# Out-degrees of a graph as a fourth product of the adjacency build, in place of a histogram of their own

## What is computed

```python
row = jnp.concatenate([edge_index[0], loop])          # edge_index = (src, dst)
deg = jax.ops.segment_sum(jnp.ones_like(row, dtype=embedding.dtype), row, num_segments=N)
deg_inv_sqrt = jnp.where(deg > 0, jax.lax.rsqrt(jnp.maximum(deg, 1.0)), 0.0)
norm = deg_inv_sqrt[row] * deg_inv_sqrt[col]
out = jax.ops.segment_sum(norm[:, None] * embedding[row], col, num_segments=N)
```

## Time and profile before

| | us |
|---|---|
| median of 3 runs | 6698.84 (6689.83 to 6706.6) |
| the profiled execution | 6690.94 |
| its span on the core | 6689.2 |
| PE, DVE, ACT, POOL busy | 5658.0, 4679.1, 1031.0, 1809.4 |
| mean granted clock of PE | 0.93 of full speed |

### The profile page before, as it was taken

The page is one execution under the profiler, slowest core; times in us unless marked ns, Lnnn a source line. Parts: engine busy times, 40 slices in busy tenths (PEclk is TensorE's granted clock), DMA queues, the critical chain, the costliest instruction groups (busy, mean ns, idle before and its releaser), DMA issues. The chain is left out here.

```text
span 6689.2 us, 122051 instructions
## 1 busy us (share of the span) xinstructions
PE 5658.0 (85%) x41983; PEld 3702.9 (55%) x41983; DVE 4679.1 (70%) x10318; ACT 1031.0 (15%) x1894; POOL 1809.4 (27%) x1887
## 2 busy tenths in 40 slices
PE   4398999999999688888888888874899959968896
PEld 3257999999999444444444444443555524433344
DVE  7789999999999788888888888868566650032003
ACT  0044444444444000000000000013000010000000
POOL 0011000000000477777777777720000002000200
PEclk5578999999999899999999999997999979989996
DMA  9555777777777433333333333340888737635862
GB/s 316 148 170 170 192 189 193 184 196 191 190 193 185 111 82 83 82 83 83 83 83 82 82 82 83 80 35 0 324 306 304 283 119 192 192 124 193 190 203 69
DMA packets 559193, 1028.57 MB, mean 154 GB/s; under 512 B 187721, under 2 KB 447710, under 8 KB 549578
## 3 DMA queue, kind: packets, MB, share of 16 engines
q1 hardware_dynamic: 486760, 872.14, 44.0%
q0 software_dynamic: 65392, 145.28, 9.7%
q10 hardware_dynamic: 6622, 6.38, 0.3%
HBM read 688.67 MB, written 387.65 MB: 161 GB/s over the span
## 5 line engine op out<-in xcount | busy, mean ns | idle before, releaser
L1272 POOL DMA_INDIRECT big<-typed_msgs,big x1712 | 1644.7, 961 | 2220.2 <-DMA big<-edge_fields 1729.8
L1319 PE MATMUL psum<-big 128*128 128x384 f32 x3424 | 1343.8, 515 | 331.0 <-DMA big<-typed_msgs,big 328.9
L1155 PE MATMUL psum<-big 128*128 128x98 bf16 x7936 | 1549.0, 272 | 49.2 <-DVE big L1137 38.2
L1156 PE MATMUL psum<-big 128*128 128x49 bf16 x7936 | 1535.7, 229 | 0.2 <-issue 0.2
L1157 PE MATMUL psum<-big 128*128 128x49 bf16 x7936 | 1534.8, 230 | 0.0
L1743 PE MATMUL psum<-big 128*128 128x512 bf16 (+1 forms) x4704 | 1003.1, 376 | 186.8 <-DMA big<-adj 186.8
L1319 PEld LDWEIGHTS psum<-big 128*128 128x128 f32 x3424 | 583.7, 190 | 756.6 <-DMA big<-typed_msgs,big 502.0
L1155 PEld LDWEIGHTS psum<-big 128*128 128x128 bf16 x7936 | 933.3, 118 | 104.1 <-DVE big L1137 78.3
L1156 PEld LDWEIGHTS psum<-big 128*128 128x128 bf16 x7936 | 945.1, 119 | 0.0
L1157 PEld LDWEIGHTS psum<-big 128*128 128x128 bf16 x7936 | 932.1, 117 | 0.3 <-issue 0.3
L1743 PEld LDWEIGHTS psum<-big 128*128 128x128 bf16 x4704 | 463.3, 99 | 721.9 <-DMA big<-adj 191.9
(11 more groups left out here) (294 smaller groups left out, 4630.4 us busy)
## 6 DMA issues: line engine op xcount, KB each, us to landing
wadj<-big SPq DMA_DIRECT2D x248, 784.0 KB, 13.0
big<-wadj SPq DMA_DIRECT2D x124, 1568.0 KB, 7.2
big<-adj SPq DMA_DIRECT2D x210, 896.0 KB, 4.7
adj<-big SPq DMA_DIRECT2D x62, 1568.0 KB, 5.3
big<-edge_feats SPq DMA_DIRECT2D x856, 64.0 KB
edge_feats<-in_edge_attr SPq DMA_DIRECT2D x1, 51562.5 KB, 163.2
big<-typed_msgs,big POOLq DMA_INDIRECT x1712
big<-edge_fields SPq DMA_DIRECT2D x856, 8.0 KB
```

The source lines that it names most:

```text
L1155: pe.matmul(to[:, 0:2 * NB], lo, hi_b[:, q, g, :, u], start=True, stop=False)
L1156: pe.matmul(to[:, NB:2 * NB], lo, w2_b[:, q, g, :, u], start=False, stop=False)
L1272: pool.indirect_dma_start(out=got4[:, h, u, :], out_offset=None, in_=typed_rows, in_offset=bass.IndirectOffsetOnAxis(ap=fld4i[:, h, u, IDX ...
L1319: last = pe.matmul(ps[h][:, 0:T * P], got4[:, h, u, :], hot4[:, h, u, :], start=(u == 0), stop=(u == U - 1))
```

## The change

The 101 batches of source histograms are removed from DVE and PE. In the build, each tile gets a fourth product, `lo.T @ hi` with 49 columns, added over all 7936 tiles into one PSUM area (`sources`, bank 7); after the last batch DVE copies it to `outdeg`. The one-hots of the build now lie tile by tile with neighbouring columns, 50 wide in place of 49 (`NE`), compared in runs of two: for this every value of the table is written twice (`tabs` and `slot_tabs` double), and a new ramp `line` is made by two iotas of POOL. PSUM areas of the build are halved to 8 tiles, and PE and ACT hand over after each half batch (four copies a batch instead of two). The destination histogram keeps its layout.

```diff
+NE = NB + NB % 2
-        slot_tabs = nc.dram_tensor("slot_tabs", (GB * P, 5 * SLOTS), BF16, kind="Internal").ap()
+        slot_tabs = nc.dram_tensor("slot_tabs", (GB * P, 2 * 5 * SLOTS), BF16, kind="Internal").ap()
...
+                pool.iota(line[:, 0:P], pattern=[[1, P]], base=0, channel_multiplier=0,
+                          allow_small_or_imprecise_dtypes=True)
+                pool.iota(line[:, P:P + NE], pattern=[[1, NE]], base=1, channel_multiplier=0,
+                          allow_small_or_imprecise_dtypes=True)
...
-                def outs(j0, j1):
-                    for j in range(j0, j1):
-                        hist_hot(dve, sloc, sbkt, HB + j, j * TT, (HB + j) % 2)
-                outs(0, AHEAD)
...
-                    link(dve.tensor_tensor(rest, w, part[0], ALU.subtract))
-                    link(dve.tensor_copy(part[1], rest))
-                    dve.tensor_tensor(part[2], rest, part[1], ALU.subtract).then_inc(s_slot_w, 1)
+                    link(dve.tensor_tensor(rest, w, part[0][:, :, 0], ALU.subtract))
+                    link(dve.tensor_copy(part[1], rest2))
+                    dve.tensor_tensor(part[2], rest2, part[1], ALU.subtract).then_inc(s_slot_w, 1)
...
-                        outs(*shares[n])
...
-                dve.wait_ge(s_hist_mm, 2 * HB)
-                link(dve.tensor_copy(outdeg, out_count))
...
-                    act.copy(tabs[:, k, 0:3, :], ps[k][:, 0:3 * SLOTS].rearrange("p (r g) -> p r g", r=3)).then_inc(s_slot_e, 1)
+                    act.copy(tabs[:, k, 0:3, :, :].rearrange("p r g c -> p (r g) c"),
+                             ps[k][:, 0:3 * SLOTS].unsqueeze(2).to_broadcast([P, 3 * SLOTS, 2])).then_inc(s_slot_e, 1)
...
+        def in_pairs(hot):
+            return hot.rearrange("p t (c r) -> p t c r", r=2)
+        def ramp_to(c0, n):
+            return line[:, c0:c0 + n].rearrange("p (c r) -> p c r", r=2).unsqueeze(1).to_broadcast([P, TT, n // 2, 2])
+        def along_slots(pairs, n):
+            return pairs.unsqueeze(2).to_broadcast([P, TT, n // 2, 2])
...
-                            at_least(dve, s_mm_b, n - 1)
-                            hi = hi_b[:, q, :, 0:NB, :]
-                            dve.tensor_tensor(hi, ramps(1, NB + 1), along_t(sbk, NB), ALU.is_equal).then_inc(s_hi_b, 1)
-                            dve.tensor_tensor(lo_b[:, q, :, :, :], ramps(0, P), along_t(sl, P), ALU.is_equal)
+                            at_least(dve, s_mm_b, n * 2 - 2)
+                            hi = in_pairs(hi_b[:, q, :, 0:NE])
+                            dve.tensor_tensor(hi, ramp_to(P, NE), along_slots(sbk, NE), ALU.is_equal).then_inc(s_hi_b, 1)
+                            dve.tensor_tensor(in_pairs(lo_b[:, q, :, :]), ramp_to(0, P), along_slots(sl, P), ALU.is_equal)
...
+                dve.wait_ge(s_mm_b, 2 * NBATCH)
+                dve.tensor_copy(outdeg, sources).then_inc(s_clear, 1)
...
-                            at_least(pe, s_adj_e, n - 1)
-                            for t in range(TT):
-                                to = made_in(q)[:, t, :]
-                                g, u = t // TU, t % TU
-                                lo = lo_b[:, q, g, :, u]
-                                pe.matmul(to[:, 0:2 * NB], lo, hi_b[:, q, g, :, u], start=True, stop=False)
-                                pe.matmul(to[:, NB:2 * NB], lo, w2_b[:, q, g, :, u], start=False, stop=False)
-                                last = pe.matmul(to[:, NB:2 * NB], lo, w3_b[:, q, g, :, u], start=False, stop=True)
-                            last.then_inc(s_mm_b, 1)
+                            for h in range(2):
+                                at_least(pe, s_adj_e, n * 2 + (h - 1))
+                                for t in range(h * HT, (h + 1) * HT):
+                                    to = made_in(h)[:, t % HT, :]
+                                    lo = lo_b[:, q, t, :]
+                                    pe.matmul(sources, lo, hi_b[:, q, t, 0:NB],
+                                              start=isinstance(n, int) and n == 0 and t == 0,
+                                              stop=isinstance(n, int) and n == NBATCH - 1 and t == TT - 1)
+                                    pe.matmul(to[:, 0:2 * NE], lo, hi_b[:, q, t, :], start=True, stop=False)
+                                    pe.matmul(to[:, NE:2 * NE], lo, w2_b[:, q, t, :], start=False, stop=False)
+                                    last = pe.matmul(to[:, NE:2 * NE], lo, w3_b[:, q, t, :], start=False, stop=True)
+                                last.then_inc(s_mm_b, 1)
```

More of the change, by code:

```diff
@@ L182, in build @@
         ramp = sb("ramp", P * TU, BF16)
+        line = sb("line", P + NE, BF16)
         big_words = (nc.sbuf_bytes_remaining // 4) // 16 * 16 - 64
@@ L337, in build @@
         in_count = ps[5][:, 0:NB]
-        out_count = ps[5][:, 64:64 + NB]
         with nc.Block() as block:
@@ L847, in build @@
         w_rest, at = cut(at, 2 * SLOTS)
-        tabs, at = cut(at, 2 * 5 * SLOTS // 2)
-        tabs = tabs.bitcast(BF16).rearrange("p (k r g) -> p k r g", k=2, r=5)
+        tabs, at = cut(at, 2 * 5 * SLOTS)
+        tabs = tabs.bitcast(BF16).rearrange("p (k r g c) -> p k r g c", k=2, r=5, c=2)
         same, at = cut(at, JB)
@@ L880, in slots_here @@
                 eng.wait_ge(s_took[(n - JB) % GR], 16 * ((n - JB) // GR + 1))
-        AHEAD = 44
-        shares = [(AHEAD + (HB - AHEAD) * n // GB, AHEAD + (HB - AHEAD) * (n + 1) // GB) for n in range(GB)]
         with nc.Block() as block:
@@ L1028, in _ @@
             def _(pe):
-                def outs(j0, j1):
-                    for j in range(j0, j1):
-                        hist_sum(pe, out_count, HB + j, (HB + j) % 2, opens=j == 0, closes=j == HB - 1)
                 def turn(b):
@@ L1054, in _ @@
                         message(n - 1)
-                    outs(*shares[n])
-        tab, at = cut(0, 2 * 5 * SLOTS // 2)
-        tab = tab.bitcast(BF16).rearrange("p (k r g) -> p k r g", k=2, r=5)
+        tab, at = cut(0, 2 * 5 * SLOTS)
+        tab = tab.bitcast(BF16).rearrange("p (k r g c) -> p k r g c", k=2, r=5, c=2)
         def hots(at, n):
             c, at = cut(at, 2 * n * TT // 2)
-            return c.bitcast(BF16).rearrange("p (k g c t) -> p k g c t", k=2, g=TG, t=TU), at
+            return c.bitcast(BF16).rearrange("p (k t c) -> p k t c", k=2, t=TT), at
         lo_b, at = hots(at, P)
-        hi_b, at = hots(at, 2 * NB)
-        w2_b, at = hots(at, NB)
-        w3_b, at = hots(at, NB)
+        hi_b, at = hots(at, 2 * NE)
+        w2_b, at = hots(at, NE)
+        w3_b, at = hots(at, NE)
+        def in_pairs(hot):
[4 more added lines that the diff above has]
+            return pairs.unsqueeze(2).to_broadcast([P, TT, n // 2, 2])
         adj_st, at = cut(at, 2 * AROW // 2)
@@ L1082, in build @@
         NBATCH = GB * BATCHES
+        HT = TT // 2
         def block_pairs(eng, body):
@@ L1091, in made_in @@
         def made_in(q):
-            return psum[:, q * 2048:(q + 1) * 2048].rearrange("p (t c) -> p t c", c=P)
+            return psum[:, q * 1024:(q + 1) * 1024].rearrange("p (t c) -> p t c", c=P)
+        sources = ps[7][:, 0:NB]
         with nc.Block() as block:
@@ L1167, in body @@
                         for b in range(BATCHES):
-                            act.wait_ge(s_mm_b, i * (2 * BATCHES) + (k * BATCHES + b + 1))
-                            act.copy(adj_st[:, k, :, b * TT:(b + 1) * TT],
-                                     made_in(b % 2)[:, :, 0:NB].rearrange("p t s -> p s t"))
-                            act.copy(wadj_st[:, k, b // 2, :, b % 2 * TT:(b % 2 + 1) * TT],
-                                     made_in(b % 2)[:, :, NB:2 * NB].rearrange("p t s -> p s t")).then_inc(s_adj_e, 1)
+                            for h in range(2):
+                                act.wait_ge(s_mm_b, i * (4 * BATCHES) + (k * (2 * BATCHES) + 2 * b + h + 1))
+                                c0 = b * TT + h * HT
+                                act.copy(adj_st[:, k, :, c0:c0 + HT], made_in(h)[:, :, 0:NB].rearrange("p t s -> p s t"))
+                                act.copy(wadj_st[:, k, b // 2, :, c0 % 32:c0 % 32 + HT],
+                                         made_in(h)[:, :, NE:NE + NB].rearrange("p t s -> p s t")).then_inc(s_adj_e, 1)
                 block_pairs(act, body)
```

21 lines of the change are left out of this document (11 added, 10 removed).

## The result

The changed kernel takes 7044.74 us (median of 4 runs, 7038.75 to 7049.9) beside 6697.33 us of the kernel before (4 runs): a ratio of 1.0518, 95% interval 1.05 to 1.0536. I had forecast 6566 us and given "slower" 0.15. The profiled execution took 7041.01 us, its span is 7039.2 us, 350 us above that of before.

| | before | after | forecast |
|---|---|---|---|
| ACT's first pick of a chunk | 329.71 | 329.24 | near 329 |
| build starts (DVE clears PSUM) | 572.25 | 560.38 | near 528 |
| build ends (before: DVE's last operation; after: copy of the out-degrees) | 2194.08 | 2538.13 | near 2061 |
| length of the build | 1621.8 | 1977.8 | 1533 |

What follows compares the result with a forecast made beforehand. In the build, half of (DVE + PE + 0.16 us) set the batch pace; after the change, DVE alone would. 6690.9 - 86 (build) - 47 (slot stage) = 6558, median 7.9 above: 6566 us, range 6520 to 6685.

Steps and rivals of the forecast that it cites:

- "slower": Chance of 0.15 that the changed kernel takes longer than the one before: D, E or a full clock drop.
- The change in the build, PE: Build: a tile's 249 neighbouring columns take PE 125 ns (bounds 105 to 244), a batch 2.23 us.
- The rest of the build's sum: Build: DVE sets the pace at 3.09 us a batch instead of 3.263, -86 us (bounds -61 to -98); ACT's copies hidden.
- rival B: Build: PE idles a third of the time and its clock falls; 6735 us if always, 6645 if half the time; chance 0.15.
- C: Build: each pair of weight load and matmul has a floor of 48 ns, pace 3.31 us a batch, 6675 us; chance 0.11.
- D: Build: the stride was not what slowed PE's stream; 244 ns a tile, 6993 us; chance 0.07.
- E: Build: DVE loses its packing of two in five operations, 2.7 us more a batch, about 7990 us; chance 0.07.
- The slot stage: Stage before the build, losing 101 source histograms: -47 us, from -11 to -63.
- The -31 for the 44 histograms ahead: Slot stage: of the 44 histograms run first, only what lies behind the edges' arrival at 329.7 us comes off, -31 us.
- The 0.77 us of PE that left each block: Slot stage: the histogram's 16 matmuls in most blocks; 0.6 us off each of 13 chunk blocks, -8 us.
- The wait that I had called the bound: Slot stage, 49 gathered blocks: ACT waits 60.0 us for table stores; 154 us instead of 162, -8 (bounds -16 to +20).
- The forecast's two terms: Build -86 us and slot stage -47 us.

Runs made afterwards that it cites:

- the turns of 1697, 1825 and 1953 instructions: Changed kernel, fourth product only for 4, 8 or 12 tiles of 16: 7464.55, 7437.01 (kernel before beside these two 7265.52) and 7110.41 us.
- the short loop: Changed kernel with PE's build loop turning over 2 batches instead of 16: 6615.71 us, 0.9868 of the kernel before; repeated, 6605.11 us, 0.987.
- the bias product: The short loop, with the slot stage's message bias product over 128 rows (127 zero) instead of one: 6570.97 us, 0.9817 of the kernel before.

## Why the prediction was wrong

**The step that failed is "The change in the build, PE".** It counted columns, pairs and handshakes of a tile, and never the instructions of a loop turn. A fourth product is a third more instructions on PE; the turn went from 1569 to 2081, over what PE keeps. The kernel before stood at most 128 instructions below the edge. No row of its profile shows that; the length of the turn has to be counted in the code. No rival had a stop of PE without a cause in data. What the runs showed in its place: with the same products and a shorter turn the build is 1540 us long, with the turn of 2081 it is 1977.8, and PE stands still for 452 us on "issue".

The Trainium skill had the means: "Runtime: NRT & Kernel Launch" (section "Instruction fetch mechanics") gives PE's instruction store as 2048 instructions, refilled in blocks of 256, and says that a taken branch to a place outside of the two blocks then held forces a fetch before PE can go on. The trace agrees with the block (16.4 KB a packet). Where the page calls the fetching along a straight stream mostly hidden, the run differs: of its 356 us of idle time on "issue" with 62 batches a turn, 320 lie away from the jumps. And a limit of 2048 would have passed the turns of 1697, 1825 and 1953 instructions, which were fetched again.

**The rest of the build's sum held.** Tile 0.12 us for the 125 ns assumed; batch 3.08 for 3.09; a word read over and over costs DVE nothing (the wide operation 1.22 us); ACT's four copies 486 and 492 ns (in the short loop), forecast 490; the doubled table hidden. With a turn that is kept, the build is 1540.2 us, against 1621.8: -82 for the forecast -86. The condition for rival B did come about, PE idle a third of the time, but the clock stood at 1.00 there; it fell only after the stops. PE waits 1.0 us in each batch of the short loop, forecast 0.9. (The profile puts this down to ACT's copy, but by the code PE needs only the copies of half a batch earlier there; DVE's last operation ends at 1003.28 and PE starts at 1003.41.) C fell with starts 0.03 us apart, D and E as above. Two sums of rivals are off without harm: E's 7990 leaves out the -86 us and should be about 7905, and half the time of B gives 6650, not 6645.

**The slot stage was mis-sized:** -12 for -47. The -31 for the 44 histograms ahead came (the first pick unmoved at 329.24), but the blocks took more in place of less: (560.38 - 329.24)/62 = 3.73 us in the mean, where the forecast had (528 - 329)/62 = 3.2. The 0.77 us of PE that left each block was taken as a gain, at the clock of the earlier trace rows. With the histogram's products gone the clock fell to 0.50 and the bias and message products took 40 to 45% longer. The wait that I had called the bound shrank on its own: ACT for the store of the table, from 57.3 us to 13.7 between 290 and 560 us, because PE was now the slowest. Its row after, which answers to the earlier trace rows:

```profile
ACT big L1001 <- DMA slot_tabs<-big: 13.7, 10, 2.8
```

ACT's copy of 768 elements takes 799 ns (forecast 0.80 us). With the clock brought back by the bias product, the slot stage gives 572.25 - 528.97 = 43 us and the whole kernel 125, 6571 us. The forecast's two terms were near in size for a kernel with two edits more than the one that was made; as a forecast of this one they were wrong. That 6571 lies so near 6566 is partly luck: the message products take 507 and 554 ns there, for 606 and 637 before, a gain that the forecast did not have in it.

## What to carry to other kernels

Count the instructions of the longest loop turn on each engine before adding one to it, PE's above all, where every small matmul is two: here 1569 were kept, 1697 weren't, and the step cost 292 us. Long idle times put down to "issue" on a stream of small matmuls, with a grown instruction queue, are the sign; a shorter turn is the cure, and turns of 8 and 2 batches cost nothing here. When work is taken away from PE, look at what its clock does to the work that stays.

## What the hardware showed that I had not expected

- A loop turn between 1569 and 1697 PE instructions is where fetching starts again at each turn. In the changed kernel it costs 452 us of stops, about a fifth at the jumps; the clock was 0.50 after the stop that was looked at.
- Beside 4.7 MB of stores, packets of instructions began 10 to 12 us apart, on idle DMA engines about 6.
- PE 100% busy with one-row and f32 products stood at 0.50; with 128 rows in place of one in a product of the same shape, it was at 0.91 in the window shown, and the two products took 554 and 507 ns in place of 849 and 923.
- PE idle a third of every batch for 1540 us had a granted clock of 1.00 (a tile in 0.12 us, as at 2.4 GHz).
- A moving bf16 operand with a step of four elements costs 0.94 ns a column, with neighbours (249 columns in 0.12 us) 0.48; the same step in the weights costs (0.146 - 0.12)/4, 6 to 7 ns a load.
